# A ring of five split weight halves and three raw weight slots in an fp32r autoencoder kernel

## The reference

```python
def reference(x, W_enc, b_enc, W_dec, b_dec):      # x 512 x 2 x 1024, W_enc 2 x 1024 x 4096, W_dec 2 x 4096 x 1024
    f = jax.nn.relu(jnp.einsum('bld,ldf->bf', x, W_enc) + b_enc)
    return jnp.einsum('bf,lfd->bld', f, W_dec) + b_dec
```

## Time and profile before

| | us |
|---|---|
| median of 3 runs | 658.13 |
| lowest, highest | 657.04, 658.8 |
| the profiled execution's own time | 658.55 |
| its span, first to last instruction | 656.8 |

### The profile page before, as it was taken

One profiled execution on the slowest core, in us unless ns is written; L12 is line 12 of the kernel. 1 busy time (PEld: TensorE's weight loads), 2 busy tenths in 40 slices (PEclk: granted clock), 3 DMA queues, 4 the chain that ended last, 5 costly groups with the idle time before them and its releaser, 6 DMA issues.

```text
span 656.8 us, 8032 instructions
## 1 busy us (share of the span) xinstructions
PE 645.6 (98%) x2904; PEld 527.9 (80%) x2904; DVE 568.8 (87%) x746; ACT 340.2 (52%) x427; POOL 17.9 (3%) x26
## 2 busy tenths in 40 slices
PE   9989999999999999999999999999999999999997
PEld 6868888888887788888888887788877888888886
DVE  5899999989999956659897599999999999998854
ACT  5655445336455454555656657445555445464452
POOL 0000100000000000000000000001100011011000
PEclk9989999999999999999999999999999999999999
DMA  8936895654545564554545465469945579589625
GB/s 331 374 129 215 235 292 205 204 197 159 177 160 199 182 212 145 193 178 163 189 144 193 146 240 185 182 220 250 275 185 193 193 229 269 199 218 315 209 99 192
DMA packets 43958, 135.81 MB, mean 207 GB/s; under 512 B 5136, under 2 KB 6160, under 8 KB 43920
## 3 DMA queue, kind: packets, MB, share of 16 engines
q1 hardware_dynamic: 40752, 124.56, 54.0%
q0 software_dynamic: 2880, 10.49, 8.4%
q10 hardware_dynamic: 288, 0.26, 0.1%
HBM read 120.61 MB, written 4.19 MB: 190 GB/s over the span
## 4 chain that ended last, share of the span: by engine, by line
PE 74%; DVE 18%; issue 3%; ACT 2%; DMA 1%; SPq 0%; DVEq 0%; ACTq 0%
PE sums L667 24%; PE sums L669 24%; PE sums L668 24%; DVE w_split L458 7%; DVE w_raw L458 4%; PE sums L724 3%; DVE forms L458 3%; DVE s_sum L458 2%; DVE place L458 1%; DMA w_raw<-w_enc 1%; ACT w_split L323 1%; ACT place L393 1%; ACT forms L339 0%; ACT place L367 0%; ACT place L380 0%
## 5 line engine op out<-in xcount | busy, mean ns | idle before, releaser
L323 ACT CAST w_split<-w_raw 128x1024 fp32r<-128x1024 f32 (+1 forms) x251 | 236.5, 947 | 279.5 <-PE sums L669 215.9
L667 PE MATMUL sums<-w_split,forms 128*128 128x512 f32 x900 | 356.0, 396 | 5.6 <-DVE w_split L458 4.9
L669 PE MATMUL sums<-w_split,forms 128*128 128x512 f32 x900 | 351.3, 390 | 0.0
L668 PE MATMUL sums<-w_split,forms 128*128 128x512 f32 x900 | 351.1, 390 | 0.0
L458 DVE TENSOR_TENSOR w_split<-w_raw,w_split 128x512 fp32r<-128x512 f32 (+1 forms) x253 | 265.3, 1084 | 59.5 <-ACT w_split L323 58.7
L667 PEld LDWEIGHTS sums<-w_split,forms 128*128 128x128 f32 x900 | 169.5, 188 | 46.2 <-issue 10.7
L669 PEld LDWEIGHTS sums<-w_split,forms 128*128 128x128 f32 x900 | 169.3, 188 | 36.0
L668 PEld LDWEIGHTS sums<-w_split,forms 128*128 128x128 f32 x900 | 169.6, 188 | 33.7
L458 DVE TENSOR_TENSOR w_raw<-w_raw 128x512 f32<-128x512 f32 x248 | 170.7, 688 | 7.2 <-DMA w_raw<-w_dec 2.9
L458 DVE TENSOR_TENSOR place<-place,sums 128x1024 f32<-128x1024 f32 (+1 forms) x26 | 29.5, 1175 | 5.9 <-PE sums L669 3.7
L458 DVE TENSOR_TENSOR forms<-place,forms 128x512 fp32r<-128x512 f32 (+2 forms) x51 | 29.1, 570 | 5.9 <-ACT forms L398 2.8
(11 more groups left out here) (24 smaller groups left out, 68.3 us busy)
## 6 DMA issues: line engine op xcount, KB each, us to landing
w_raw<-w_dec SPq DMA_DIRECT2D x96, 512.0 KB, 4.2
w_raw<-w_enc SPq DMA_DIRECT2D x93, 512.0 KB, 4.0
place<-place POOLq DMA_DIRECT2D x20, 512.0 KB, 8.0
w_raw<-w_enc SPq DMA_DIRECT2D x32, 256.0 KB, 2.7
w_raw<-w_dec SPq DMA_DIRECT2D x32, 256.0 KB, 3.0
place<-xT SPq DMA_DIRECT2D x8, 512.0 KB, 10.2
outT<-place SPq DMA_DIRECT2D x12, 256.0 KB, 2.1
outT<-place SPq DMA_DIRECT2D x6, 128.0 KB, 2.3
```

The lines of the kernel that those rows point to most:

```text
L323: nc.scalar.copy(split(s, q, 0), w_pos(s, 2 * q, n)).then_inc(hi_done, 1)
L667: nc.tensor.matmul(out[:, m, :], v_hi, w_hi[:, cols], start=start, stop=False)
L668: nc.tensor.matmul(out[:, m, :], v_lo, w_hi[:, cols], start=False, stop=False)
L669: last = nc.tensor.matmul(out[:, m, :], v_hi, w_lo[:, cols], start=False, stop=stop)
```

## The change

`RAW` becomes 3. `w_split` becomes a ring of five halves, used in the order of 2s + q, and `hi` waits for the block that used the same half five halves earlier. The raw slots shrink by 8 KB a partition and the split halves grow by 8 KB. `load_w` isn't edited, but its wait follows RAW: the load of step s now waits for the low halves of step s-3, from step 3 on, and this moves the waits in front of everything that SP issues behind them.

```diff
-    RAW = 4
+    RAW = 3
+    HALVES = 5
...
-        w_split = sbuf("w_split", [P, 2, 2, 2, 2 * C], F32R)
+        w_split = sbuf("w_split", [P, HALVES, 2, 2 * C], F32R)
...
-            return w_split[:, s % 2, q, part, 0:n * C]
+            return w_split[:, (2 * s + q) % HALVES, part, 0:n * C]
...
-                if s >= 2:
-                    act.wait_ge(multiplied, BLOCKS[s - 2][q])
+                if 2 * s + q >= HALVES:
+                    before = 2 * s + q - HALVES
+                    act.wait_ge(multiplied, BLOCKS[before // 2][before % 2])
```

## The result

| | us | against before |
|---|---|---|
| before | 658.46 (median of 4) | |
| changed | 676.50 (median of 4, 676.11 to 677.39) | ratio 1.0275, 95% interval 1.0259 to 1.0291 |
| changed, a second set of runs | 678.02 (median of 4) | 1.0298, 1.0273 to 1.0323 |

The forecast was 11.3 us slower and the measured change is 18.0. The sign and the places are right, the size is not: 676.5 is the upper end of the stated range, and the second set lies above it. The profiled execution took 677.39 us with a span of 675.3, against 658.55 and 656.8.

The account below looks back on a forecast made before the run. The PE was taken to bound the kernel, busy 645.6 of 656.8 us, with the DVE just behind. Terms 2.4 + 2.7 + 2.8 + 3.7 - 0.3 = 11.3 us, laid on the median 658.13, gave 669.4 us; range 663.5 to 676.5.

Parts of the forecast that it names:

- Loads late beside the folds, by one step's lead: Fold stretches at 82, 450, 540, 590 us: loads issued one step later land late, costing 2.4, 2.7, 2.8, 3.7 us.
- Nearly none elsewhere: Outside about 88, 459, 547 and 590 to 600 us, the DVE would hardly wait for raw weights.
- The landing of load s+1 read from before as that of load s: Every step: load s+1's old landing, if after the start of step s's sums, gives the new DVE wait.
- First folds, 2.4 us: Stretch at 82 us: load 14 late by 4.05 us, 1.65 us free, cost 2.4 us, upper bound 3.9.
- No slack in the second and third stretch: Stretches at 450 and 540 us: nothing absorbs the late loads 90 and 106, cost 2.7 and 2.8 us.
- Fourth folds, 3.7 us: Stretch at 590 us: loads 114 and 116 late, 5.3 us in all, 1.6 free; cost 3.7, from 1.8 to 5.6.
- The clock left out of the sum: Half clock after a PE wait over 2 us, first or last stretch: 1.7 us, only in the range.
- The fifth half, 0.3 us: Ahead of step 81, an earlier high half shortens the PE's 0.31 us wait: gain 0.3 us, bounds 0 and 1.8.
- Quiet stretches at zero: Steps away from folds: hidden with forms, some 0.2 us late without, losing only DVE lead; cost zero.
- the first and the fourth: Rivals: fifth half wins, 656.3 us, chance 0.04; loads land as in quiet stretches, no change, 658 us, chance 0.04.
- the second (the engines share in turns from the start): Rival, fold stretches: loads land 2 us sooner without the dead 2 us; 3.4 us slower, 661.5 us, chance 0.07.
- the third: Rival: three slots bind in quiet form-free steps too, about 10 us more, 679 us, chance 0.05.

Follow-up runs that it names:

- the first experiment: Three raw slots with the old four split halves, against the kernel before: 675.03 us, ratio 1.0234.
- the second experiment: The kernel before, four slots and four halves, each load waiting for the low halves of step s-3 instead of s-4: 676.04 us, ratio 1.0264.
- 5 and 6: The 20 folds cut to 16 elements a partition, in the kernel before: 658.71 us; in the changed kernel: 662.35 us.
- the third experiment: The changed kernel with ten matmuls of zeros added before each of steps 89, 105 and 116: 677.57 us, ratio 1.0285.
- the eleventh: The changed kernel run once more, unedited: 678.02 us.
- the tenth experiment: The kernel before with each fold issued only when the one before it has landed: 665.09 us, ratio 1.0100.
- the seventh: The changed kernel with each fold issued only when the one before it has landed: 669.53 us, ratio 1.0158.
- the fourth experiment: The kernel before with twelve matmuls of zeros added before step 3: 657.73 us, ratio 0.9992.

## Why the prediction was right, and where it was wrong

The mechanism held. The step that failed is the price of a stretch with folds: it was worked out from one late load (two in the fourth), with its landing read from one execution. The four terms 2.4, 2.7, 2.8 and 3.7 measured 4.4, 3.9, 4.1 and 5.5, and the first is off the most.

- **Loads late beside the folds, by one step's lead**: right. Experiments 1 and 2 show that the issue time is the whole mechanism, 5 and 6 that four fifths of the loss need the folds. "Nearly none elsewhere" was wrong for the DVE's waits, 20 of 32, and right for the PE's.
- **The landing of load s+1 read from before as that of load s**: a fair estimate, low by half a microsecond. It said 2.7 and 2.8 us at steps 90 and 106, and the eight measured waits have a mean of 3.2. It takes one execution's landings for a quantity that ranges from 1.9 to 4.9.
- **First folds, 2.4 us**: this step failed most, by 2.0. The load of step 9, ahead of the folds, was in no term and no bound. It was late by 2.64 us at 61.80 in the changed kernel; the folds began 2.6 us later (74.55 instead of 71.96, POOL's timeline), and then came the loads of steps 13 and 14, late by 1.25 and 2.30. That is 6.2 us instead of 4.05, and the slack that hid the rest, 1.8 us, is near the 1.65 forecast. The prediction's own rule would have found load 9. In the trace of before the second half of load 10 went out at 54.78, and the sums of step 9 started at 58.62:

```profile
DMA to landing us min/median/max: 5.9/5.9/5.9
```

```profile
58.62 2.14 DVE L458 TENSOR_TENSOR w_raw<-w_raw 128x512 f32<-128x512 f32 x3
```

Landed at 60.7, it is late by 2.0 us. It gives 1.25 for load 13, as measured, where I had put 1.5 into the upper bound only. Load 9 was late in every other profiled run with this lead too, by 0.6 to 2.6 us, with and without folds. What slows the loads near 55 us stays open.
- **No slack in the second and third stretch**: right, and I should have drawn more from it. Where the DVE is without a pause, every late load counts in full, also the small ones: 0.38 and 0.37 us ahead of the 3.13, and 0.26 ahead of the 3.43. The sum had one load for each stretch. With these and the measured 3.13 and 3.43, 2.7 becomes 3.9 and 2.8 becomes 3.7 of the 4.1.
- **Fourth folds, 3.7 us**: the interpolated load of step 116 was late by 0.02 us, not 3.4 (it waited 1.08 us for load 115 first and 0.75 for 114). The big one was load 117, late by 4.05; the plain rule names it, since load 118 landed at 604.6 in the trace of before and the sums of step 117 started at 599.31. The cost of 5.5 lies at the upper bound of 5.6, but by another load than the one I worked it out for. That term's working was wrong and its bounds right.
- **The clock left out of the sum**: right as a number, for a reason that I didn't give. The half clock came three times, 5.1 us in the records, and by the third experiment under 1 us of it reached the end. It came in the second and third stretch, where the prediction didn't look for it, and not in the first.
- **The fifth half, 0.3 us**: too small for the medians, but seen in its place. In the eleventh and the third experiment, which have it, the PE gains 0.4 us on before at step 81; in the first, with four halves, it gains nothing there. In the profiled run of the changed kernel the wait ahead of step 81 is 0.48 us, not gone, and 0.5 us was lost at step 78. Elsewhere there is nothing: the DVE's waits for ACT fall from 58.7 us (39 times) to 28.6, of which the late loads alone make a part (40.2 in the first experiment), and the DVE then waits for PE results (10.7 us where it was 3.7) or for loads.
- **Quiet stretches at zero**: nearly. The profiled run of the changed kernel has 0.4 us there, the kernels without folds 2.2 to 3.5 in all.

The rivals' fate: the first and the fourth fell; the second (the engines share in turns from the start) fell with landings of 11 us; the third holds for 2 to 3.5 us. Of the turns a part is true: between 453 and 460 us in the trace of before the loads' queue and the folds' moved 255 and 253 packets. It is the start that doesn't fit, and part of the two microseconds of the earlier trace rows passes before any load's first packet, which comes 1.0 us after its issue in quiet stretches too (0.95 to 0.98, seven loads from step 96 on). In the same place behind the issue of a quiet load (485.40), from 486.0 to 488.0 us, that queue moved 142 packets instead of 4:

```profile
q1 hardware_dynamic: 142, 0.55, 81.8%
```

The fit of the Trainium skill that the prediction cites ("DMA: Bandwidth & Descriptors", "Anatomy of one DMA") is given there for transfers by POOL's software queue, which here are the folds and not the loads. Its estimate of 3.2 us for 512 KB stands against 8.0 for a fold (median of before), and 4.1 to 4.2 for a load in a quiet stretch.

The terms that were too small add up: 2.0 + 1.2 + 1.3 + 1.8 for the folds, 0.45 for a start that is not the change's, and 0.7 for the stretch in which I had a gain. That is 7.4 us, within rounding what lies between 18.6 and 11.3.

## What to carry to other kernels

A buffer slot is worth the issue time that it gives, so read its price from the landing of the next load in the trace of before, at the step where this one is wanted, and do it for every load, in stretches without slack and ahead of them too, not for the worst. Where transfers of another queue run, take the spread from several executions: a margin of half a microsecond there is no margin. Space for a further stage helps only if the engine behind it has idle time in the same stretch; the list of waits tells how much, not whether it is on the path.

## What was not expected of the hardware

A load whose packets start while three folds are in flight gets almost nothing at first, and beside one at a time it lands in at most 8.8 us instead of 11.4. Transfers in sequence also took longer altogether: in the tenth experiment the last fold of the fourth stretch went out at 607.37 and was late by 4.04 us, where before the last pair had gone out at 593.57.

The length of a PE wait alone doesn't tell whether half clock follows. It followed waits of 2.32 to 2.49 us in the changed kernel, of 1.96 in the second experiment (97.9 to 101.3 us) and of 1.89 in the first (619.7 to 623.1), and didn't follow waits of 2.21 in the changed kernel, 2.28 in the eleventh, and 3.05 and 3.07 at step 3 of the first and the seventh. What decides it, these runs don't show. Nor has it one price: it cost almost nothing where the DVE was still the later engine behind the wait, 1.5 us at the start of the kernel before (the fourth experiment), and 2.4 us at step 118 of the tenth experiment, where the PE set the pace.
